# Setup of a post-LN attention and FFN layer: ln_w's load moved behind Wo, x issued first, chunk 0's squares on VectorE, clip logarithms on GpSimd, waits split by operand

## The reference

```python
r = sigmoid(x @ Wr.T); k = x @ Wk.T; v = x @ Wv.T
log_decay = log(clip(sigmoid(decay), 1e-07))
scale = exp(t * log_decay)                      # t = 0 .. 2047
state = cumsum(k * v / clip(scale, 1e-10), axis=1) * scale
x = layernorm(x + rmsnorm(r * state, ln_w) @ Wo.T)
h = gelu(x @ bin(w1).T + b1)
x = layernorm(x + h @ bin(w2).T + b2)
```

## Time and profile before

| what | value |
|---|---|
| median of 3 runs | 835.58 us (835.35 to 835.84) |
| profiled execution: span | 833.5 us |
| profiled execution: its own whole time | not recorded; the median lies 2.1 us above the span |
| PE busy | 811.5 us, 97% of the span |
| DVE busy | 754.4 us, 91% |
| ACT busy | 679.1 us, 81% |
| POOL busy | 335.0 us, 40% |
| landing of a 512 KB load of x, median of 32 | 3.9 us |

### The profile page before, as it was taken

The page is one execution under the profiler, slowest core; times in us unless marked ns, Lnnn a source line. Parts: engine busy times, 40 slices in busy tenths (PEclk is TensorE's granted clock), DMA queues, the critical chain, the costliest instruction groups (busy, mean ns, idle before and its releaser), DMA issues.

```text
span 833.5 us, 16874 instructions
## 1 busy us (share of the span) xinstructions
PE 811.5 (97%) x5365; PEld 527.3 (63%) x5365; DVE 754.4 (91%) x1400; ACT 679.1 (81%) x971; POOL 335.0 (40%) x569
## 2 busy tenths in 40 slices
PE   6989999999999999999999999999999999999996
PEld 4555666666666666666666666666666666666663
DVE  6987999999999999999999999999999999999877
ACT  7886888888888888888888888888888888887775
POOL 3344333444333344333344333344433344433354
PEclk9999999999999999999999999999999999999999
DMA  8513553444553434554434554434454334444313
GB/s 247 104 30 77 128 114 90 99 103 101 126 126 81 103 93 101 126 126 90 107 80 107 120 126 101 100 80 108 113 126 107 94 87 109 106 101 101 77 26 101
DMA packets 169845, 86.27 MB, mean 103 GB/s; under 512 B 130144, under 2 KB 165472, under 8 KB 169824
## 3 DMA queue, kind: packets, MB, share of 16 engines
q1 hardware_dynamic: 148304, 52.97, 27.6%
q0 software_dynamic: 4608, 16.78, 10.4%
q10 hardware_dynamic: 16912, 16.26, 5.7%
HBM read 20.45 MB, written 16.78 MB: 45 GB/s over the span
## 4 chain that ended last, share of the span: by engine, by line
PE 90%; DVE 4%; ACT 2%; POOL 2%; DMA 1%; issue 1%; POOLq 0%; DVEq 0%; ACTq 0%; SPq 0%
PE ps_r L355 29%; PE ps_o L478 25%; PE ps_f L428 18%; PE ps_o L382 6%; PE ps_r L428 6%; PE ps_o L387 3%; PE ps_s L362 2%; DVE hid_lo L966 1%; DMA x_t<-x_st 1%; DMA x_in<-in_L_attn_x_dram 1%; ACT hid L657 0%; DVE u L917 0%; DVE u_st L925 0%; POOL root L1256 0%; ACT hid_hi L692 0%
## 5 line engine op out<-in xcount | busy, mean ns | idle before, releaser
L478 PE MATMUL ps_o<-w2T,hid_hi 128*128 128x256 f16 x992 | 218.9, 273 | 3.3 <-DVE hid_lo L966 2.9
L478 PE MATMUL ps_o<-w2T,hid_lo 128*128 128x256 f16 x992 | 218.8, 273 | 0.0
L355 PE MATMUL ps_r<-x_t,proj_hi 128*128 128x512 f16 x768 | 197.1, 379 | 1.4 <-DVE proj_lo L1042 1.2
L657 ACT ACTIVATE hid<-ps_f,b1c,f_scale 128x512 f32<-128x512 f32 x192 | 145.3, 774 | 54.7 <-PE ps_f L428 49.6
L428 PE MATMUL ps_f<-x_t,w1T 128*128 128x512 f16 x768 | 182.0, 379 | 2.3 <-DVE x_t L950 1.3
L1244 POOL TENSOR_TENSOR y_sqs<-y_sq 128x512 f32<-128x512 f32 x32 | 46.7, 1461 | 315.7 <-ACT y_sq L632 315.7
L966 DVE SCALAR_TENSOR_TENSOR hid_lo<-hid,hid_scale,hid_hi 128x1024 f16<-128x1024 f32 (+1 forms) x136 | 160.3, 1221 | 1.2 <-ACT hid_hi L692 0.6
L355 PEld LDWEIGHTS ps_r<-x_t,proj_hi 128*128 128x128 f16 x768 | 74.7, 98 | 91.3 <-issue 2.6
L692 ACT ACTIVATE hid_hi<-hid,hid_scale 128x2048 f16<-128x2048 f32 (+2 forms) x72 | 128.0, 1779 | 3.3
L428 PEld LDWEIGHTS ps_f<-x_t,w1T 128*128 128x128 f16 x768 | 75.0, 98 | 80.4 <-issue 2.6
L355 PE MATMUL ps_r<-x_t,proj_lo 128*128 128x512 f16 x384 | 114.2, 379 | 0.0
(11 more groups left out here) (176 smaller groups left out, 1380.4 us busy)
## 6 DMA issues: line engine op xcount, KB each, us to landing
x_in<-in_L_attn_x_dram SPq DMA_DIRECT2D x32, 512.0 KB, 3.9
res<-b_row POOLq DMA_DIRECT2D x32, 512.0 KB, 4.6
out_dram<-res ACTq DMA_DIRECT2D x31, 512.0 KB, 3.1
w_in<-in_L_ffn_w_dram SPq DMA_DIRECT2D x2, 1024.0 KB, 10.1
x_t<-x_st SPq DMA_TRANSPOSE x59, 4.3
b_row<-in_L_ffn_b_dram SPq DMA_DIRECT2D x1, 512.0 KB, 13.1
proj_in<-in_L_attn_Wk_dram SPq DMA_DIRECT2D x1, 256.0 KB, 5.2
proj_in<-in_L_attn_Wv_dram SPq DMA_DIRECT2D x1, 256.0 KB, 5.4
```

The source lines that it names most:

```text
L355: last = nc.tensor.matmul(ps_r[:, m, :], w[:, m, dc, ec * P:(ec + 1) * P], xx[:, :, dc, :], start=(n == 0), stop=(n == 3 * DC - 1))
L478: last = nc.tensor.matmul(o_tok[:, tt, :], hh[:, hc, tt * P:(tt + 1) * P], w2T[:, :, hc, :], start=(hc == 0 and n == 0), stop=(hc == HC - ...
L657: nc.scalar.activation(hid[:, hc, :], f1_bank[hc % NF], ACT.Gelu, bias=b1c[:, hc:hc + 1], scale=f1_scale[:, hc:hc + 1]).then_inc(s_gelu, 1)
```

## The change

It does six things. The sizes of all tiles and the numbers of matmuls stay.

- SP issues all of x's first chunk, the projections, x's second chunk, Wo, then ln_w (before on ACT's queue), w1, w2 and x's third chunk ahead of its eight semaphore increments.
- The squares of chunk 0, and their sum, are one DVE instruction in place of an ACT one; it stands where the logarithms of the clip table stood.
- These logarithms are eight POOL instructions of 512 elements in place of two DVE ones of 2048, behind x's first scale and ahead of the undoing ones.
- ACT takes the exponential of the first part of the clip table behind the first weight's high part, no longer ahead of x's.
- PE makes six transposes of x ahead of the sum of the squares in place of four and writes all eight to banks 1 and 2 of `ps_r`; m = 0 still goes to bank 0, m = 1 and 2 to banks 1 and 2.
- PE's first `R` waits for x's high part and the weight's high part first, for x's low part ahead of the third matmul, and for the weight's low part ahead of the fifth (m = 0); for m = 1 and 2 only the wait for the weight's low part moves.

```diff
@@ SP
-            for n in range(CPB):
-                sp.sem_inc(s_stored[n], 16)
-            sp.sem_inc(s_zout, TT)
...
             load(0, 0, 0)
             for n, w in enumerate((Wk, Wv, Wr)):
                 sp.dma_start(proj_in[:, n], ...).then_inc(s_proj_in[n], 16)
             load(1, 0, 1)
             sp.dma_start(wo_in[:, :, :], ...).then_inc(s_wo_in, 16)
+            sp.dma_start(lnw_c[:, :], ln_w.rearrange("(c p) -> p c", p=P),
+                         allow_slow_non_contiguous=True).then_inc(s_lnw_in, 16)
             sp.dma_start(w1_in[:, :, :], ...).then_inc(s_w1_in, 16)
             sp.dma_start(w2_in[:, :, :], ...).then_inc(s_w2_in, 16)
             load(2, 0, 2)
+            for n in range(CPB):
+                sp.sem_inc(s_stored[n], 16)
+            sp.sem_inc(s_zout, TT)
...
@@ PE, R
-                pe.wait_ge(s_xl, c + 1)
+                if not first:
+                    pe.wait_ge(s_xl, c + 1)
...
                         if first and not ec:
-                            pe.wait_ge(s_setup_ev, m + 1)
+                            pe.wait_ge(s_proj_hi, m + 1)
+                            if m:
+                                pe.wait_ge(s_xl, c + 1)
...
+                            if first and not ec and not m and n == DC:
+                                pe.wait_ge(s_xl, c + 1)
+                            if first and not ec and n == 2 * DC:
+                                pe.wait_ge(s_setup_ev, m + 1)
@@ PE, prologue, and the banks
-        x_bank, ... = [ps_r, ps_o, ps_f], ...
+        x_bank, ... = [ps_r[:, 1:3, :], ps_o, ps_f], ...
-                transposes(x_bank[0][:, 0:DC, :], x_in[0], 0, (0, 1))
+                transposes(x_bank[0][:, 0:DC, :], x_in[0], 0, (0, 1, 2))
                 sum_xbound(0)
-                transposes(x_bank[0][:, 0:DC, :], x_in[0], 0, (2, 3)).then_inc(s_tx, 1)
+                transposes(x_bank[0][:, 0:DC, :], x_in[0], 0, (3,)).then_inc(s_tx, 1)
@@ ACT
-            act.dma_start(lnw_c[:, :], ...).then_inc(s_lnw_in, 16)
...
-            xsq(0, 0, 0, first=True)
...
-                act.wait_ge(s_clip, DC)
+                act.wait_ge(s_clip, DC * n + DC)
...
             def prologue():
-                clip_table(0)
                 xh(0, 0)
                 proj_split_hi(0)
+                clip_table(0)
                 proj_split_hi(1)
@@ DVE
-            dve.wait_ge(s_const, 1)
-            dve.wait_ge(s_setup_a, 2)
-            for dc in range(DC):
-                nc.vector.tensor_scalar(clip_g[:, dc, :], steps[:, :], dec_c[:, 2, dc:dc + 1], -LOG_CLIP, ALU.mult,
-                                        ALU.min).then_inc(s_clip, 1)
+            dve.wait_ge(s_x_in[0], 16)
+            nc.vector.scalar_tensor_tensor(out=x_sq[:, :, :], in0=x_in[0][:, :, :], scalar=1.0, in1=x_in[0][:, :, :],
+                                           op0=ALU.mult, op1=ALU.mult,
+                                           accum_out=bounds[:, DC:DC + 1]).then_inc(s_xsq, 1)
@@ POOL
             scales(0, 0)
+            pool.wait_ge(s_setup_a, 2)
+            for n in range(CPB):
+                for dc in range(DC):
+                    part = slice(n * CH, (n + 1) * CH)
+                    nc.gpsimd.tensor_scalar(clip_g[:, dc, part], steps[:, part], dec_c[:, 2, dc:dc + 1], -LOG_CLIP,
+                                            ALU.mult, ALU.min).then_inc(s_clip, 1)
             pool.wait_ge(s_winv, 1)
             unscales(0, 0)
```

More of the change, by code:

```diff
@@ L165, in postln_layer_kernel @@
         o_last = ps_r[:, 0:2, :].rearrange("p a (b d) -> p (a b) d", d=D)
-        x_bank, x_split = [ps_r, ps_o, ps_f], [(x_hi, x_lo), (x1_hi, x1_lo), (x_hi, x_lo)]
+        x_bank, x_split = [ps_r[:, 1:3, :], ps_o, ps_f], [(x_hi, x_lo), (x1_hi, x1_lo), (x_hi, x_lo)]
         ps_bounds = ps_s[:, TT:TT + DC + 1]
@@ L257, in load @@
                 sp.dma_start(x_in[j][:, :, :], x_v[c]).then_inc(s_x_in[j], 16)
+            load(0, 0, 0)
+            for n, w in enumerate((Wk, Wv, Wr)):
+                sp.dma_start(proj_in[:, n], w.rearrange("(c p) d -> p c d", p=P)).then_inc(s_proj_in[n], 16)
+            load(1, 0, 1)
+            sp.dma_start(wo_in[:, :, :], Wo.rearrange("(c p) d -> p c d", p=P)).then_inc(s_wo_in, 16)
+            sp.dma_start(lnw_c[:, :], ln_w.rearrange("(c p) -> p c", p=P),
+                         allow_slow_non_contiguous=True).then_inc(s_lnw_in, 16)
+            sp.dma_start(w1_in[:, :, :], w1.rearrange("(c p) d -> p c d", p=P)).then_inc(s_w1_in, 16)
+            sp.dma_start(w2_in[:, :, :], w2.rearrange("(c p) h -> p c h", p=P)).then_inc(s_w2_in, 16)
+            load(2, 0, 2)
             for n in range(CPB):
@@ L659, in gelu, with xsq @@
                                          scale=f1_scale[:, hc:hc + 1]).then_inc(s_gelu, 1)
-            def xsq(c, b, j, first=False, looped=False):
+            def xsq(c, b, j, looped=False):
                 act.wait_ge(s_x_in[j], 16 * b + 16)
@@ L665, in xsq @@
                     act.wait_ge(s_bounds, c - 2)
-                elif not first:
+                else:
                     act.wait_ge(s_xbounds, c)
@@ L697, in _ @@
                           allow_slow_non_contiguous=True).then_inc(s_decay_in, 16)
-            act.dma_start(lnw_c[:, :], ln_w.rearrange("(c p) -> p c", p=P),
-                          allow_slow_non_contiguous=True).then_inc(s_lnw_in, 16)
             act.wait_ge(s_decay_in, 16)
```

8 lines of the change are left out of this document (removed).

## The result

| kernel | median | runs | ratio to before, 95% interval |
|---|---|---|---|
| before | 835.71 us | 4, 835.35 to 835.84 | |
| changed | 846.48 us | 4, 846.03 to 847.04 | 1.0131, 1.0117 to 1.0146 |

The change makes the kernel 10.8 us slower; the prediction said 1.8 us faster. The profiled execution of the changed kernel spans 845.2 us, 11.7 more than before.

What follows compares the result with a forecast made beforehand. TensorE is always busy from 80 us, so only its start can move, gated by x's first load; a shift there carries on whole. Terms -0.5 - 0.8 + 0.3 + 0 - 0.8 = -1.8 from 835.58 gave 833.8 us, range 832.8 to 835.2.

Steps and rivals of the forecast that it cites:

- Part 3: Clip-table logarithms on GpSimd, part of the table later on ScalarE: eight of 0.69 us, hidden, so 0.
- The row taken as the bad end: A similar GpSimd form in the tail, up to 1.20 us beside VectorE; at that length +1.5 us in all, 837.1.
- GpSimd holds k_sb: Rival: logarithms longer than 0.79 us each delay x_scl and so chunk 0's k_sb; up to 837.1 us; chance 0.09.
- Part 1: First loads: x issued at 0.72 (-0.5 us), its transfer 4.2 in place of 5.00 (-0.8); -1.3 us.
- the first rival: Smaller gain: decay's packets slow x as ln_w's did, x still takes 5.0 us; about -0.8, 834.8 us; chance 0.26.
- Part 2: Chunk 0's squares on VectorE: SBUF access clash with GpSimd's decay_f costs 0 to 0.7 us, taken as +0.3.
- Part 4: TensorE's first projection waits split by operand: VectorE loses idle times of 0.42, 0.16 and 0.20 us; -0.8 us.

Runs made afterwards that it cites:

- e6: Kernel before with only the waits split by operand, and chunk 0's transposes one PSUM bank further; 834.26 us, ratio 0.9987.
- e1: Kernel before with eight extra GpSimd instructions of 512 elements in various forms behind the first x_scl, results unread; 842.24 us, one run.
- e4: Kernel before with only the clip logarithms on GpSimd, minimum included, and ScalarE's first table part later; 846.66 us, ratio 1.0129.
- e7: Kernel before with only the load order changed: x issued first, ln_w behind Wo; 837.99 us, ratio 1.0027.
- parts 1 and 2 without it: The change with waits as before instead of split by operand, and the minimum left out (clip not applied); 835.80 us, ratio 1.0005.

## Why the prediction was wrong, point by point

**Part 3 is the step that failed: "eight instructions of the form of decay_f, 0.69 us each".** decay_f multiplies and adds; the logarithm multiplies and takes a minimum. I matched the shape, type and engine, not the operation. The row taken as the bad end, at 1.20 us, is also two multiplications, so it was no bound either. Measured: 1.99 us.

**The mechanism was the rival "GpSimd holds k_sb", at the wrong price.** Its threshold was 0.79 us each. Put the measured 1.99 into its own sum: 8 x (1.99 - 0.79) - 1.8 = +7.8, 843.4 us; with the 2.08 us from start to start it is +8.5, 844.1. The change with TensorE kept busy took 843.98, 8.9 more than the kernel before beside it. So the mechanism is right in size, if not in every term (the gain of 1.8 in it was 1.1 at the loop scans). What that sum lacked is a second price: TensorE's clock, 1.8 us. ScalarE's two waits for the table parts, which the prediction did not name, cost nothing of their own here, since k_sb waits for x_root longer still. The prediction's evidence against this rival was thin: y_inv at 29.16 lay beside kvg (28.48, 0.75 us long) for 0.07 us only.

**Part 1, -1.3 us: half right.** x was issued at 0.74, as said. Its transfer took 4.8 us (4.7 to 5.0 in the nine profiles with this issue), not 4.2, near the upper end that I had given; decay's packets took ln_w's place beside x, as the first rival had it, and decay itself landed 4.5 us after its issue at 0.73, where the page of before has 2.1. Both are what the Trainium skill (DMA: Bandwidth & Descriptors, Queues, rings and completion order) has of queue rows that take turns, and the run with decay ahead (3.6 us for x, 2.1 for decay) agrees. How much a neighbour costs is not settled by this: with the loads as before, ln_w beside x, its transfer took 5.0 us in the profile of before, 4.7 in e6 and 4.3 in e1 and e4, so the 5.0 that the sum started from was one execution's.

The path was wrong too. In the kernel before, ScalarE, which loads its Exp table behind the decay's logarithm, was free for x's squares only at 6.24, the moment at which x landed; e1 and e4, with x 0.7 us earlier, have x_scl only 0.12 earlier. Part 2 takes the squares off ScalarE, but VectorE's squares and GpSimd's decay_f both stand behind the clip of the decay (VectorE, 5.62). So in the changed kernel the chain of waits starts with decay's load and not with x's:

```profile
0.73 4.54 DMA dec_c<-in_L_attn_decay_dram
...
5.99 2.17 POOL decay_f L1333 x2
```

The prediction let decay's landing move to "no earlier than now" and priced nothing for it; part 1 alone shows that 2.4 us there cost 2.7 where the squares are still on ScalarE and the logarithms on VectorE.

**Part 2, +0.3 us: right in size, other in kind.** The squares took 1.22 us unhindered, and the first decay_f waited for them: by tile, changed kernel (ns: minimum, median, maximum):

```profile
L1333 POOL TENSOR_SCALAR decay_f<-steps,dec_c x2: 689/1086/1482, 6.0 to 7.5; 128x512 f32<-128x512 f32 x2
```

One of the two took 0.79 us more than the other; in e7, without the squares beside it, the pair took 1.37 us at nearly the same time (5.88). It fits the exclusive lock of the Trainium skill (SBUF — State Buffer, SBUF: two separate sides), held by the one that starts first: the squares started at 5.70, decay_f at 5.99, and 0.93 us of the squares were left. And x_scl behind them came at 8.13. ScalarE's x_t waited 0.26 us for that, and VectorE's 0.32.

**Part 4, -0.8 us: held.** The waits named went, and it is worth a little more, 1.07 us alone.

**The sum without part 3's slip:** the kernel without the minimum took 833.55 us (833.22 to 835.23) where the prediction's sum said 833.8. That is luck. At the loop scans this kernel is 1.1 us early and not 1.8, and the terms were not these: part 4 alone gave 1.2, and parts 1 and 2 without it 0.45 in place of 1.0. Behind part 4 they added 0.35 at x_t (-1.62 against -1.27) and nothing at the loop scans (-1.11 against -1.23). So a gain at the first products is not always carried on whole, as the prediction had it: this kernel is still 1.45 us early at 137 us and 1.10 at 162, and between them TensorE waits for a DMA transpose (0.17 us at 142.76), where before has no such wait.
